# Two pairs of PSUM buffers for the attention output, and an output projection spread evenly over the head pairs

## The reference

```python
# layer 0
xn = _layernorm(x, axis=-1)
s = _L0_attn_ref(xn, Wq, Wk, Wv, Wo)      # 16 query heads, 4 kv heads, width 64, rotary, no mask
g = _silu(_L0_ffn_ref(xn, ...))           # mixture of experts: 16 experts (top 4 of 16) + 2 shared
x = x + s * g
# layer 1
xn = _layernorm(x, axis=-1)
s = _L1_attn_ref(xn, W_qkv, b_qkv, W_out, b_out)   # 16 heads of 64, causal
g = _silu(_L1_ffn_ref(xn, w_gate, w_up, w_down))   # dense ffn, int weights, width 3072
x = x + s * g
```

## Time and profile before

| what | us |
|---|---|
| median of 2 runs | 5006.74 |
| the two runs | 4931.22 and 5082.27 |
| the profiled execution | 4933.55 |
| its span, slowest core (core 7) | 4932.0 |
| spans of the eight cores | 4901.6 to 4932.0 |
| PE, DVE, ACT, POOL busy | 3659.1, 1285.7, 1329.8, 282.1 |

### The profile page before, as it was taken

The page is one execution under the profiler, slowest core; times in us unless marked ns, Lnnn a source line. Parts: engine busy times, 40 slices in busy tenths (PEclk is TensorE's granted clock), DMA queues, the critical chain, the costliest instruction groups (busy, mean ns, idle before and its releaser), DMA issues.

```text
span 4932.0 us, 44326 instructions; the slowest of 8 cores (4901.6 to 4932.0 us)
## 1 busy us (share of the span) xinstructions
PE 3659.1 (74%) x14712; PEld 1450.5 (29%) x14712; DVE 1285.7 (26%) x2076; ACT 1329.8 (27%) x1573; POOL 282.1 (6%) x522
## 2 busy tenths in 40 slices
PE   2256667799999999976777777743999966667675
PEld 0022222344434444432222222211444422222221
DVE  3433320033033023122222222225101023443332
ACT  1100000011011011004656565521111101445563
POOL 1000000000000000000000000011101000000000
PEclk9578887999999999988898989865999999889998
DMA  2257777644434434430011111134444420122121
GB/s 78 65 161 194 211 196 180 170 140 145 154 120 145 148 136 143 145 92 9 13 37 32 37 33 37 28 95 103 73 75 71 73 47 9 32 43 56 29 56 45
DMA packets 139086, 450.92 MB, mean 91 GB/s; under 512 B 15568, under 2 KB 15728, under 8 KB 122480
## 3 DMA queue, kind: packets, MB, share of 16 engines
q0 software_dynamic: 73632, 218.42, 21.4%
q1 hardware_dynamic: 65232, 229.67, 13.5%
HBM read 490.23 MB, written 73.40 MB: 114 GB/s over the span
## 4 chain that ended last, share of the span: by engine, by line
PE 52%; DMA 16%; DVE 15%; ACT 10%; issue 5%; DVEq 1%; SPq 0%; POOL 0%; ACTq 0%; POOLq 0%
ACT a16t L1490 9%; PE pst L745 8%; PE pst L759 8%; PE pst L861 4%; PE pb L861 4%; DMA a32t<-l_u 4%; PE pb L1002 3%; PE pb L1437 3%; PE pst L1460 3%; PE pst L938 2%; PE pst L1465 2%; PE pst L1354 2%; PE pst L949 2%; DMA a16t<-s_g 2%; PE pb L1442 2%
## 5 line engine op out<-in xcount | busy, mean ns | idle before, releaser
L1490 ACT ACTIVATE a16t<-pst 128x1024 bf16<-128x1024 f32 x832 | 852.6, 1025 | 609.4 <-PE pst L1465 538.4
L745 PE MATMUL pst<-xn_sb,a16t 128*128 128x512 bf16 x2304 | 594.2, 404 | 189.5 <-DVE a16t L693 160.5
L759 PE MATMUL pst<-xn_sb,a16t 128*128 128x512 bf16 x2304 | 564.0, 389 | 0.0
L1437 PE MATMUL pb<-a16t 128*65 128x512 bf16 x832 | 342.6, 412 | 290.5 <-DVE a16t L1578 119.5
L780 DVE TENSOR_TENSOR a32t<-a32t,pst 128x512 f32<-128x512 f32 x256 | 175.9, 687 | 1139.6 <-PE pst L759 1133.8
L1460 PE MATMUL pst<-a16t 128*128 128x512 bf16 x832 | 352.0, 423 | 163.0 <-DVE a16t L1399 103.8
L772 ACT ACTIVATE a32t<-pst 128x512 f32<-128x512 f32 x288 | 172.1, 598 | 1109.1 <-PE pst L745 1109.1
L745 PEld LDWEIGHTS pst<-xn_sb,a16t 128*128 128x128 bf16 x2304 | 226.2, 102 | 505.7 <-issue 291.7
L1465 PE MATMUL pst<-a16t 128*128 128x512 bf16 x832 | 350.1, 421 | 0.0
L1442 PE MATMUL pb<-a16t 128*65 128x512 bf16 x832 | 343.5, 413 | 0.0
L759 PEld LDWEIGHTS pst<-xn_sb,a16t 128*128 128x128 bf16 x2304 | 231.7, 101 | 294.3 <-issue 46.2
(11 more groups left out here) (156 smaller groups left out, 2794.2 us busy)
## 6 DMA issues: line engine op xcount, KB each, us to landing
a16t<-s_g POOLq DMA_DIRECT2D x108, 512.0 KB, 5.0
a16t<-s_u SPq DMA_DIRECT2D x108, 512.0 KB, 3.6
a32t<-l_u SPq DMA_DIRECT2D x32, 1024.0 KB, 10.5
a16t<-s_d SPq DMA_DIRECT2D x27, 1024.0 KB, 5.2
a16t<-s_d POOLq DMA_DIRECT2D x27, 1024.0 KB, 5.2
s_g<-a16t SPq DMA_DIRECT2D x36, 512.0 KB, 7.8
s_u<-a16t SPq DMA_DIRECT2D x36, 512.0 KB, 8.5
s_d<-a16t SPq DMA_DIRECT2D x18, 1024.0 KB, 8.1
```

The lines of the kernel that those rows point to most:

```text
L745: li = t.matmul(pb[gp_][:, :], a16t[:, o_gb[wp] + hc * 256 + ici * 128: o_gb[wp] + hc * 256 + ici * 128 + 128], xn_sb[:, hc * T + tc * TC: ...
L759: li = t.matmul(pb[up_][:, :], a16t[:, o_ub[wp] + hc * 256 + ici * 128: o_ub[wp] + hc * 256 + ici * 128 + 128], xn_sb[:, hc * T + tc * TC: ...
L1437: t.matmul(pb4[0:65, :], a16t[:, o_vtm + kc * 65 * nvh + kva * 65: o_vtm + kc * 65 * nvh + kva * 65 + 65], a16t[:, o_pt[kp4]:o_pt[kp4] + T ...
L1490: return s.activation(a16t[:, o_pt[kp4]:o_pt[kp4] + 2 * TC], pst[kp][:, 0:1024], AF.Exp, scale=0.125)
```

## The change

Three things are changed in `phase_C`.

1. The product with V goes to pb4 and pb5 in pairs with even number, and to pb6 and pb7 in pairs with odd number (`pi = qi % 2`). The epilogue of a pair uses the pair's own two tiles. The first product of a pair now depends on the multiplications of the pair two before it, `pv[("normd", pi)]`, and on the last fusion.
2. The output projection writes pb6 for an even `fc` and pb5 for an odd one (`pbo_of`). Its first matmul of each block gets new dependencies: the two multiplications (and the reciprocals) of the pair whose tiles it borrows, `pv[("normd", 1 - fc % 2)]`.
3. The 80 units become 8 groups, one for each pair. `start_group` issues the load of weights at the start of the pair (for p = 0 at kc = 1), `emit_unit` puts one matmul behind each product from kc = 1 on, and `finish_group` emits at the end of the pair what is left of the matmuls, and then the end of the group. No unit is emitted at kc = 0 any more, nor the two extra ones at the end of a pair.

```diff
+            def pbo_of(fc):
+                return pb6 if fc % 2 == 0 else pb5
...
             def make_oproj_units(qcd, norm_deps):
-                units = []
+                groups = []
                 for fc in range(NHC):
...
+                    units = []
...
                                 return t.matmul(
-                                    pb[6 + fc % 2][:, :],
+                                    pbo_of(fc)[:, :],
...
                                 dm += [prvb] + norm_deps
+                                dm += pv.get(("normd", 1 - fc % 2), [])
+                                dm.append(pv.get(("rcps", 1 - fc % 2)))
...
+                        pv[("lastfuse",)] = op_fuse
...
+            def start_group():
+                if curg[0] is None and pend:
+                    g = pend.pop(0)
+                    g[0]()
+                    curg[0] = g
+                    curg[1] = list(g[1:-1])
 
             def emit_unit():
-                if pend:
-                    pend.pop(0)()
+                if curg[0] is not None and curg[1]:
+                    curg[1].pop(0)()
+
+            def finish_group():
+                if curg[0] is not None:
+                    while curg[1]:
+                        curg[1].pop(0)()
+                    curg[0][-1]()
+                    curg[0] = None
...
+                    pi = qi % 2
+                    av_a, av_b = (pb4, pb5) if pi == 0 else (pb6, pb7)
...
                         if kc == 0:
-                            dav += [v_last, op_ms] + pv.get(("normd",), [])
+                            dav += [v_last, op_ms, pv.get(("lastfuse",))]
+                            dav += pv.get(("normd", pi), [])
+                            if qi == 1:
+                                dav += [op_kevl, op_vevl]
...
                         if kc == 1:
                             flush_epi()
+                            start_group()
                         if kc >= 1:
                             emit_av(kc - 1)
-                        emit_unit()
+                            emit_unit()
...
                     op_avl = emit_av(nkc - 1)
-                    emit_unit()
-                    emit_unit()
+                    finish_group()
```

More of the change, by code:

```diff
@@ L602, in phase_A @@
             res = dict(xn_last=prev[("xnl", NTC - 1)])
+            res["xn_tc"] = [prev[("xnl", t_)] for t_ in range(NTC)]
             res["lasts"] = [res["xn_last"]]
@@ L605, in phase_A @@
                 res["c_last"] = ct_ops[-1][0]
+                res["c_tc"] = [ct_ops[4 * t_ + 3][0] for t_ in range(NTC)]
                 res["lasts"].append(res["c_last"])
@@ L1429, in phase_C, with emit_av, f_av @@
                     flush_epi1()
+                    start_group()
                     exp_ops = {}
-                    def emit_av(kc, kva=kva, kvb=kvb, nkc=nkc, qc=qc, p=p):
+                    def emit_av(kc, kva=kva, kvb=kvb, nkc=nkc, qc=qc, p=p,
+                                av_a=av_a, av_b=av_b, pi=pi, qi=qi):
                         kp4 = kc % 2
                         pt_d = exp_ops[kc][1]
-                        def f_av(t, kc=kc, kp4=kp4, kva=kva, kvb=kvb, nkc=nkc):
-                            t.matmul(pb4[0:65, :],
+                        def f_av(t, kc=kc, kp4=kp4, kva=kva, kvb=kvb, nkc=nkc,
+                                 av_a=av_a, av_b=av_b):
+                            t.matmul(av_a[0:65, :],
                                      a16t[:, o_vtm + kc * 65 * nvh + kva * 65:
@@ L1442, in f_av @@
                             return t.matmul(
-                                pb5[0:65, :],
+                                av_b[0:65, :],
                                 a16t[:, o_vtm + kc * 65 * nvh + kvb * 65:
@@ L1556, in f_bc @@
                                 def f_bc(t):
-                                    t.matmul(pb4[:, :], cst16[:, B_BR0:B_BR0 + 128],
+                                    t.matmul(av_a[:, :], cst16[:, B_BR0:B_BR0 + 128],
                                              a16t[:, o_nrm:o_nrm + TC],
@@ L1590, in phase_C @@
                     epi1_pend[0] = mk_epi1()
-                while pend:
-                    emit_unit()
+                while pend or curg[0] is not None:
+                    start_group()
+                    finish_group()
             flush_epi1()
             flush_epi()
-            while pend:
-                emit_unit()
+            while pend or curg[0] is not None:
+                start_group()
+                finish_group()
             stores = [ops[("stx", 0)], ops[("stx", 1)]]
```

29 lines of the change are left out of this document (18 added, 11 removed).

## The result

The changed kernel is faster, by a little: the ratio of its time to the time before is 0.9908, with a 95% interval from 0.9886 to 0.9931. That excludes no change, but it is less than the 2% which the prediction took as what a measurement can tell. The profiled execution took 4879.83 us, 53.7 us less than the 4933.55 of the one before; the median of 13 runs is 4887.59. (Both kernels have executions in which the cores of a die run at a lower clock and take some per cent longer; the plain median of 11 runs of the kernel before, 5082.27 us, is one of these, and the ratio leaves them out.)

The account below looks back on a forecast made before the run. No single engine was taken as the bound; limits change by stage, with ACT limiting inside a pair. Gains of 12.6 + 12 + 3.5 + 10.5 + 9 = 47.6 us from 4933.55 gave 4886 us, range 4838 to 4945.

Parts of the forecast that it names:

- step on TensorE's clock: Clock in all 62 pairs: a third of them shifting level is 29 us either way; taken as zero.
- Layer 0, first chunk: Seven pairs without projection matmuls: the product starts 1.8 us earlier in each, 12.6 us gained.
- Layer 0, chunks two to four: 24 pairs with projection: product hidden and fewer matmuls behind the multiplication, 4.0 us a chunk, 12 us gained.
- the step's own terms: Layer 0's later chunks: product 0.43 us, two matmuls saved 0.43, uncovered projection matmul 0.216, one inside a step 0.08.
- The moved wait: Later chunks: PE's wait for the multiplications remains at the projection's line, shortened to about 1.3 us.
- Layer 1, first chunk: Seven pairs: product 1.7 us earlier, but DVE's second mask still holds the next; 0.5 us each, 3.5 us gained.
- Layer 1, second chunk: Fusion no longer between copies and multiplications: 1.45 us for each of seven pairs, 0.3 for the first, 10.5 us gained.
- The fusion's cover: Layer 1's second chunk: eight query matmuls (1.89 us) hide the moved fusion's 1.5 us; uncovered, 1.5 us a pair lost.
- Layer 1, chunks three and four: Two matmuls saved at pair ends, product hidden, fusions out of the masks: 5 + 4 = 9 us gained.
- The slower one: Projection matmuls in low-clock first blocks of some 17 pairs, more pairs at low clock: 13 us slower, 4947 us; chance 0.10.
- Nothing in projection pairs: The wait just moves and matmuls eat the savings; only both layers' first chunks gain, 4917 us; chance 0.17.
- The first rival: The whole wait goes in all 62 pairs, 112 us plus 5 us at pair ends: 4817 us; chance 0.08.

Follow-up runs that it names:

- e4: The changed kernel plus useless matmuls in PE's idle time ahead of the scores; ratio 0.9732 to the kernel before, profiled execution 4792.4 us.
- e5: The kernel before the change plus the same number of useless matmuls, written into pst0; ratio 0.9902, 4882.76 us.
- e2: The changed kernel with the projection's matmuls starting from the third key block of a pair instead of the second; 4772.52 us, ratio 0.9688.
- e1: The kernel before plus the grouped projection alone, products staying in pb4 and pb5, projection in pb6 and pb7; 4916.75 us, ratio 0.9974.

## Why the prediction came out as it did

The total is close, 4886 us forecast and 4879.83 in the profile (median 4887.59), or 47.6 us of gain against 53.7. That is in part luck: of the parts of the sum, two gave 15.4 us more than forecast and one 7.6 less. The prediction's main reading, that the wait stays in the queue and stands one instruction later wherever a projection matmul is in the pair, was right. What failed is its step on TensorE's clock, "I take zero", and it shows in layer 0's later chunks. Its own sign of being wrong came up there: the granted clock of pairs was to move by no more than 0.03, and in layer 0's first two chunks it moved by 0.07 up and 0.04 down.

- *Layer 0, first chunk.* Forecast 12.6 us, measured 20.3. The wait is 1.88 us a pair at full clock (e4, e5), so 13.2 of the 20.3. The other 7 go with the clock, 0.85 to 0.92, by subtraction. Without any filling, two pairs at 0.94 differ by 1.6 us (28.84 in the earlier trace rows and 27.26 at the end of this text). The forecast sign of a third exponential within 1.0 us came true (0.70), and that of the pairs' length (27 to 28.5) nearly: seven of the eight took 26.97 to 27.30 us, the first 29.78.
- *Layer 0, chunks two to four.* Forecast 12 us, measured 4.4 (1.2, -0.2, 3.4), and 0.9 by the medians of the cores. This is where the step failed: the clock was put at nothing, while the counts were right. At full clock the step's own terms hold: 1.13 us for a pair that had 14 matmuls, where its terms sum to 0.43 + 0.43 + 4 x 0.08 = 1.18, and 0.28 us lost for a pair that had none, where they give 0.216 - 7 x 0.08 = -0.34. With 4.4 and 3.6 such pairs that is 4.0 us a chunk, the figure of the prediction. At the lower granted clocks the terms hold as well: a pair that had 14 matmuls goes from 32.09 us at 0.84 to 30.70 at 0.83, 1.39 less, and one that had none from 30.23 to 30.70, both at 0.83, 0.47 more. What changed is how many pairs are that low. Before, 10 of the 23 pairs of these chunks had 0.83 or 0.84 and 8 had 0.94; after, 20 have 0.83 and one 0.94. Ten more low pairs, at up to the 1.39 us between the two pairs of equal work in the earlier trace rows, are worth up to 14 us by that estimate, enough for the 7.6 us that are missing of 12. The cause of the drop is shown only as far as e2 and e4 go: the later start and the filling each bring the clock back, to 0.92 and 0.99.
- *The moved wait* was seen right from the order: PE waits 25 times in each layer at the projection. Its length there is 0.87 us at the low clock and 1.30 at full clock; the forecast had about 1.3. All pairs of a chunk take nearly the same time, as forecast: 29.1 to 31.0 us in layer 0's second.
- *Layer 1, first chunk.* Forecast 3.5, measured 1.4, at a clock that fell from 0.85 to 0.76. DVE's order bound it as said: at a clock of 1.00 a pair takes 13.18 us before and 13.11 after, where the forecast had 0.15 us left.
- *Layer 1, second chunk.* Forecast 10.5, measured 11.6. The start of one of its pairs, answering to the earlier trace rows:

```profile
4294.48 0.69 DVE L1301 TENSOR_TENSOR a32t<-a32t 128x512 f32<-128x512 f32 x1
4294.75 0.38 PE L1381 MATMUL pst<-xn_sb,a16t 128*128 128x512 bf16 x1
...
4295.35 0.74 DVE L1435 TENSOR_SCALAR a16t<-pst,cst 64x512 bf16<-64x512 f32 x1 [0.18 <-DVE a32t L1301]
...
4298.86 0.38 PE L1597 MATMUL pb<-a16t,cst 128*128 128x512 bf16 x1
...
4299.34 0.68 DVE L1607 TENSOR_TENSOR a16t<-a16t,pb 64x512 bf16<-64x512 bf16 x1 [0.84 <-PE pb L1597]
...
4300.97 0.38 PE L1249 MATMUL pb<-a16t 128*128 128x512 bf16 x1 [1.30 <-DVE a16t L1615]
```

The multiplication now starts 0.48 us after the spread matmul, not 1.57. The fusion's cover just holds: the query's DVE operation is released by the fusion, 0.18 us after its end, and the query's last matmul ended at about the same moment. e1 shows that most of this gain does not need the second pair of tiles.
- *Layer 1, chunks three and four.* Forecast 9, measured 16.7 (13.2 by the medians of the cores). The sizes were taken from layer 0 and were too small; the fusions that no longer stand among the masks are the likely rest, but no run isolates them.
- *The rivals.* The slower one named the right place, projection matmuls in the blocks where the clock is low, and a clock that falls by more than 0.03; it took back part of the gain but never the whole. "Nothing in projection pairs" is close to what layer 0 did, and far from layer 1. The first rival, the wait gone everywhere, was wrong for the changed kernel as it stands, and 4817 us were not reached. Its order, with two pairs of tiles, left one user in the bank still being read, and when e2 moved that user by one block the gain became 3.1%. The Trainium skill (Perfetto Trace Analysis, Optimizing Tensor Performance) says that independent matmul groups should rotate through different PSUM banks. By that rule, e2 agrees.

## What to carry to other kernels

When a wait is taken from an instruction, look at the next instruction in the same queue that touches the freed buffer: the wait is there now, and it may need only to stand one step later. Sum a change at one clock first, and then ask whether the engine's idle pieces get longer or shorter, since the clock can pay more than the wait, or take it back. Work that must share an idle buffer belongs behind the last reader of that buffer, not behind the first moment at which the schedule has room.

## What the hardware showed that was not expected

- In the changed kernel PE's granted clock hardly moves from pair to pair: seven pairs of layer 0's first chunk take 27.0 to 27.3 us one after the other at 0.94, and those with projection 30.69 us again and again at 0.83. In the kernel before, pairs with the same work had both values. These two pairs of the changed kernel differ by 3.4 us, for eight matmuls that occupy 8 x 0.216 = 1.7 us:

```profile
2341.25:2368.51 27.26, 20.33 (x75) 6.82 (x75) 6.18 (x9) 18.62 (x20) 0.53 (x1) 0.94 0.07 10
2664.08:2694.78 30.70, 23.76 (x83) 8.06 (x83) 7.58 (x12) 18.63 (x20) 1.06 (x2) 0.83 0.17 35
```

- More work made the program shorter: 512 matmuls of no use in layer 0 and 224 in layer 1 took the changed kernel from 4879.83 to 4792.4 us. Four a pair did nothing in layer 0 (0.92 with and without), sixteen gave 0.99 to 1.00. Why sixteen suffice and four do not is open.
